# A layernorm's casts moved from GpSimd to ScalarE, and a broadcast copy from ScalarE to VectorE

## The reference

```python
def attn(x):                       # phi(y) = elu(y) + 1, heads of 64
    q = phi(heads(x @ Wq.T + bq)); k = phi(heads(x @ Wk.T + bk))
    v = heads(x @ Wv.T + bv)
    kv = einsum('bhtd,bhtm->bhdm', k, v)
    z = 1.0 / (einsum('bhtd,bhd->bht', q, k.sum(axis=2) + EPS) + EPS)
    out = einsum('bhtd,bhdm,bht->bhtm', q, kv, z)
    return out @ Wo.T + bo
def ffn(x):                        # weights dequantized by 1/127
    return (silu(x @ wg.T) * (x @ wu.T)) @ wd.T
x = layernorm(x + attn(x))         # mean, variance over 1024 features
x = layernorm(x + ffn(x))
```

## Time and profile before

| | |
|---|---|
| median of 2 runs | 5113.15 us (5107.51 to 5118.79) |
| profiled execution, its time | 5102.1 us |
| profiled execution, span of the slowest core (4) | 5100.2 us |
| spans of the 8 cores | 5089.6 to 5100.2 us |
| busy share of the span | PE 72%, DVE 34%, ACT 18%, POOL 11% |
| mean granted clock of PE | 0.83 of 2.4 GHz |

### The profile page before, as it was taken

How to read it: one execution, slowest core, us unless ns; L and a number is a source line. 1 busy time by engine, 2 the same in 40 slices (tenths; PEclk the granted TensorE clock), 3 DMA queues, 4 the chain that set the end, 5 groups by cost and what they waited for, 6 DMA issues and landing times.

```text
span 5100.2 us, 43631 instructions; the slowest of 8 cores (5089.6 to 5100.2 us)
## 1 busy us (share of the span) xinstructions
PE 3689.1 (72%) x15184; PEld 1435.9 (28%) x15184; DVE 1708.7 (34%) x2435; ACT 931.7 (18%) x1659; POOL 554.6 (11%) x668
## 2 busy tenths in 40 slices
PE   1587647677655876799964877699973877699982
PEld 0232212222211322244421322244430322244430
DVE  0124422222232144333333133433333134433333
ACT  2232211011111232111111232111111232211111
POOL 0003210000021013100011012200012012200002
PEclk9787768888877977899976977799985987799995
DMA  4100022222212000010102000010103000001001
GB/s 161 40 0 1 1 74 75 75 75 75 72 49 84 1 1 0 25 50 25 50 33 99 1 1 1 25 50 26 50 10 122 1 1 0 25 26 50 26 25 66
DMA packets 69676, 199.99 MB, mean 39 GB/s; under 512 B 4933, under 2 KB 4934, under 8 KB 60248
## 3 DMA queue, kind: packets, MB, share of 16 engines
q1 hardware_dynamic: 56504, 153.15, 8.5%
q10 hardware_dynamic: 12960, 44.05, 2.5%
HBM read 144.75 MB, written 52.43 MB: 39 GB/s over the span
## 4 chain that ended last, share of the span: by engine, by line
PE 59%; DVE 13%; ACT 8%; DMA 7%; POOL 7%; issue 5%; DVEq 0%; ACTq 0%; SPq 0%; POOLq 0%
PE ps L774 13%; PE ps L753 12%; PE ps L799 12%; PE ps L415 5%; PE ps L620 5%; PE ps L370 4%; DVE x L254 4%; DVE wstage L250 4%; DMA wstage_i<-wu 3%; PE ps L529 3%; POOL arena L189 2%; DMA wstage_i<-wg 2%; POOL arena L187 2%; POOL h_arena L189 1%; DVE h_arena L785 1%
## 5 line engine op out<-in xcount | busy, mean ns | idle before, releaser
L753 PE MATMUL ps<-y_bf,arena 128*128 128x512 bf16 x3072 | 710.3, 388 | 181.9 <-POOL arena L722 74.5
L774 PE MATMUL ps<-y_bf,arena 128*128 128x512 bf16 x3072 | 706.0, 387 | 106.4 <-DVE arena L722 106.4
L799 PE MATMUL ps<-h_arena,arena 128*128 128x512 bf16 x3072 | 694.1, 379 | 35.8 <-DVE h_arena L785 35.8
L785 DVE SCALAR_TENSOR_TENSOR h_arena<-ps,h_arena 128x512 bf16<-128x512 f32 x384 | 265.5, 691 | 1044.9 <-PE ps L774 1041.8
L811 DVE SCALAR_TENSOR_TENSOR x<-ps,x 128x512 f32<-128x512 f32 x768 | 530.2, 691 | 183.6 <-PE ps L799 113.6
L763 ACT ACTIVATE h_arena<-ps 128x512 bf16<-128x512 f32 x384 | 229.1, 597 | 1857.1 <-PE ps L753 1857.1
L415 PE MATMUL ps<-wk_bf,arena 128*128 128x512 bf16 x1024 | 290.4, 433 | 294.2 <-ACT arena L439 177.7
L187 POOL CAST arena<-x 128x512 bf16<-128x512 f32 x160 | 98.2, 614 | 3594.6 <-DVE x L628 1661.6
L753 PEld LDWEIGHTS ps<-y_bf,arena 128*128 128x128 bf16 x3072 | 304.4, 99 | 574.5 <-issue 229.3
L774 PEld LDWEIGHTS ps<-y_bf,arena 128*128 128x128 bf16 x3072 | 303.7, 99 | 493.1 <-issue 144.8
L799 PEld LDWEIGHTS ps<-h_arena,arena 128*128 128x128 bf16 x3072 | 293.7, 98 | 420.6 <-issue 80.4
(11 more groups left out here) (78 smaller groups left out, 2705.8 us busy)
## 6 DMA issues: line engine op xcount, KB each, us to landing
x<-x SPq DMA_DIRECT2D x16, 2048.0 KB, 8.0
out<-x SPq DMA_DIRECT2D x16, 2048.0 KB, 6.9
arena<-stash_wg SPq DMA_DIRECT2D x18, 1024.0 KB, 4.8
arena<-stash_wd SPq DMA_DIRECT2D x18, 1024.0 KB, 6.9
arena<-stash_wu ACTq DMA_DIRECT2D x18, 1024.0 KB, 4.8
wstage_i<-wg SPq DMA_DIRECT2D x48, 256.0 KB, 2.7
wstage_i<-wd ACTq DMA_DIRECT2D x48, 256.0 KB, 2.6
wstage_i<-wu SPq DMA_DIRECT2D x48, 256.0 KB, 2.6
```

What stands on the lines that cost most here:

```text
L753: e.matmul(ps[b_][:, 0:512], slots[sl_][:, 512 * kk + 128 * gg:512 * kk + 128 * (gg + 1)], y_bf[:, T * kk + t_:T * kk + t_ + 512], start=( ...
L774: e.matmul(ps[b_][:, 0:512], slots[sl_][:, 512 * kk + 128 * gg:512 * kk + 128 * (gg + 1)], y_bf[:, T * kk + t_:T * kk + t_ + 512], start=( ...
L785: e.scalar_tensor_tensor(h_arena[:, 512 * gg:512 * (gg + 1)], ps[b_][:, 0:512], S127, h_arena[:, 512 * gg:512 * (gg + 1)], ALU.mult, ALU.m ...
L799: e.matmul(ps[b_][:, 0:512], slots[sl_][:, 1024 * ss + 128 * mm:1024 * ss + 128 * (mm + 1)], h_arena[:, 512 * ss:512 * (ss + 1)], start=(s ...
```

## The change

Three operations move to another engine, and the waits with them.

- The cast of the statistics (one of the two POOL operations for each chunk, in LN1 and LN2) becomes an ACT copy. It has its own waits on DVE and on PE, and PE waits for ACT as well as for POOL.
- The cast to y_bf in LN1 becomes an ACT copy. The wait of PE on POOL ahead of the FFN is taken out; PE waits for ACT there already.
- The copy of the broadcast z from bank 3 to SBUF becomes a DVE copy. PE's next broadcast waits for DVE instead of ACT, and bank 3 is handed to the next tile's Q projection by DVE's count.

```diff
             for m in range(NCH):
                 sa, sb_ = scr[m % npair]
+                p.wait("scalar", dve, src_ready_dve)
+                p.wait("scalar", pe, hist[m % npair])
+                p.op("scalar", lambda e, mm=m, t_=t0, d_=sa: e.copy(
+                    d_[:, :], x32[:, T * mm + t_:T * mm + t_ + 512]), inc=act)
+                cst = act.n
                 p.wait("gpsimd", dve, src_ready_dve)
                 p.wait("gpsimd", pe, hist[m % npair])
-                p.op("gpsimd", lambda e, mm=m, t_=t0, d_=sa: e.tensor_copy(
-                    d_[:, :], x32[:, T * mm + t_:T * mm + t_ + 512]))
                 p.op("gpsimd", lambda e, mm=m, t_=t0, d_=sb_: e.tensor_mul(
...
+                p.wait("tensor", act, cst)
                 p.wait("tensor", pool, sq)
...
                 if want_ybf:
-                    p.wait("gpsimd", dve)
-                    p.op("gpsimd", lambda e, mm=m, t_=t0: e.tensor_copy(
+                    p.wait("scalar", dve)
+                    p.op("scalar", lambda e, mm=m, t_=t0: e.copy(
                         y_bf[:, T * mm + t_:T * mm + t_ + 512],
-                        x32[:, T * mm + t_:T * mm + t_ + 512]), inc=pool)
+                        x32[:, T * mm + t_:T * mm + t_ + 512]), inc=act)
...
                     p.wait("tensor", act, z_ready)
-                    p.wait("tensor", act)
+                    p.wait("tensor", dve, zb_ps3_free)
...
-                    p.wait("scalar", pe, zmm)
-                    p.wait("scalar", dve, zb_free[c % 2])
-                    p.op("scalar", lambda e, cc=c:
-                         e.copy(zb[cc % 2][:, :], ps[3][:, 0:512]), inc=act)
-                    zev = act.n
+                    p.wait("vector", pe, zmm)
+                    p.wait("vector", dve, zb_free[c % 2])
+                    p.op("vector", lambda e, cc=c:
+                         e.tensor_copy(zb[cc % 2][:, :], ps[3][:, 0:512]),
+                         inc=dve)
+                    zev = dve.n
+                    zb_ps3_free = dve.n
...
-                    p.wait("vector", act, zev)
+                    p.wait("vector", dve, zev)
...
-                q_free[3] = act.n
+                q_free_d[3] = zb_ps3_free
...
-            p.wait("tensor", pool)
```

More of the change, by code:

```diff
@@ L500, in build_nc @@
             a_mult = [0] * NCH
+            zb_ps3_free = 0
             stats_free = kv_ready
```

## The result

The changed kernel takes 5028.9 us (median of 11 runs) where the kernel before takes 5183.9 (10 runs). The ratio is 0.979, with a 95% interval from 0.975 to 0.983. That is clearly faster, but the interval holds 0.98, so these runs do not settle whether it is by more than 2%. The spans of single cores are the sharper measure: in the profiled executions core 0 took 5099.0 us before and 4978.7 after, 120 us less, a ratio of 0.976.

A forecast was written before the change was run, and what follows sets the result against it. Serial stretches on other engines while PE stands still were taken as the bound. Terms -72.3 - 62.1 + 12.8 + 21 - 7.1 = -107.7 us take the profiled 5102.1 to 4994, the median 5113 to 5005; 8-in-10 range 4972 to 5042.

The forecast's parts named there:

- The bound: Whole kernel: PE stands still in stretches paced by a serial walk over other engines, such as POOL's layernorm statistics.
- Statistics, LN2: Layernorm behind the FFN, 16 times: casts on ACT shorten the statistics from 13.74 to 9.22 us, saving 72.3 us.
- rival C: Statistics: ACT's cast slows POOL's multiply to 1.93 us, about +110 us in all, 5223; chance 0.05.
- rival D: Statistics gain nothing, chunks staying 1.55 us apart by an unseen limit; +26.7 us, 5140; chance 0.04.
- Statistics, LN1: Layernorm behind the attention, 16 times: statistics take 9.86 us with two scratch pairs, saving 3.88 each, 62.1 in all.
- The ring's arithmetic: LN1's two scratch pairs: multiply m waits until PE has read pair m-2; long matmuls make two chunks take 2.30 us.
- The copy of z: Chunk loop, 128 copies: DVE's copy takes 0.69 us, a step 1.56 instead of 1.46; +12.8 us.
- Rival A: DVE's z copy runs as from SBUF, 0.43 us; sum -140.5, 4972; chance 0.07.
- The hand-over: Apply's start to next tile's denominators: y_bf casts on ACT delay the Q projection, +1.75 us, 12 times, +21.
- Rival B: Next tile's Q projection gets no cover under the apply: +8.6 instead of +1.75, 82 us more, 5087; chance 0.05.
- The FFN's start: Apply's start to FFN's first matmul: 13.5 instead of 15.27 us, saving 1.77, 4 times, 7.1.

The follow-up runs named there:

- denser statistics in the kernel before: Kernel before with one more matmul, result unused, for each chunk of the statistics, POOL still doing both operations; core 0 took 5106.3 us against 5103.
- the pause filled: Changed kernel with 30 more matmuls, results unused, at each of the 12 hand-overs; core 0 took 4956 us, 27 less than the changed kernel.

## Why the prediction was off, and what of it held

**The bound.** Right. The statistics stood on the path in all 32 layernorms, and a cast taken off POOL shortened the path by its whole spacing: a chunk takes 1.00 us instead of 1.55.

**Statistics, LN2.** The spacing of two multiplies was taken as 0.99 and is 0.99 to 1.00; the multiply beside ACT takes 1.039 us, so rival C (ACT and POOL hinder each other) fell, and rival D too. The mis-sized term is the 1.25 us between the last multiply's end and ACT's read. It was read from a tile with long matmuls and kept; it measured 0.83, in all 16 tiles. The spacing, slightly above 0.99, takes some of this back, and 16 times 0.36 us is the 5.8 us that this term missed.

**Statistics, LN1.** This is the step that failed: "I take the first four starts at the short spacing and the rest at the long one". The ring's arithmetic was right (2.30 said, 2.35 measured; the four tiles in which it bound took 10.1 us on the mean), but the length of the matmuls was copied from the kernel before, where they came two to each 1.55 us. With a chunk a microsecond PE has more to do in the same time, and in 12 of 16 tiles the matmuls stayed short to the end. The denser statistics in the kernel before show that more work on PE by itself makes tiles stay or turn short; why it was 12 tiles and not 16 stays open. A saving of 3.88 us a tile was expected, 4.60 measured: 11.5 us in all, the largest miss of the sum.

**The copy of z.** Right in size: 0.69 was taken, 0.691 measured. The step was 1.52 instead of 1.56: the copy starts 0.70 us after its broadcast (median), where 0.73 was taken. Rival A (0.43 us) fell. The page VectorE: DVE Perf Modes of the Trainium skill, section Why PSUM operands drop a tier, gives f32 from PSUM no fast mode, and the 691 ns agree. The cost table of that page of the Trainium skill would have put the copy at 658 ns, an estimate, which is 33 ns short.

**The hand-over.** Right in mechanism: PE restarted 14.65 us after the apply's start (14.67 said), the projection split 32 and 32 with a pause of 6.5 to 7.4 us (near 8 said). The size was +2.37 instead of +1.75, and the term that was too small is what the pause adds to the matmuls behind it: 3.0 or 1.4 us over 6.92 was taken, 2.1 on the mean of the 12, and it measured 2.7 (9.66 us). The prediction paired the longer and the shorter of today's two kinds of restart with the same kind after the change; measured, 11 of the 12 lie from 23.7 to 24.9 and one at 23.0, where before 5 of the 12 were of the longer kind (22.6 to 22.9) and 7 of the shorter (21.1 to 21.6). The bounds given there, +0.5 and +3.2, don't follow from its own terms either: without long matmuls 14.67 + 6.92 = 21.6 is 0.5 less than the mean of 22.1, and with twice as many it is 26.0, 3.9 more. With the pause filled 21.76 was measured. Rival B (no cover at all) fell.

**The FFN's start.** Right: 13.77 for 13.5 said, and the load of the up weights stayed covered: PE waits for no DMA at the up matmuls (line 780).

**The total.** The ratio of 0.979 is what was said (4994 over 5102), but that agreement is partly luck. On core 0 the change gave 120 us and not 107.7, and even this holds two errors that work against each other: 17.3 us too little from the statistics, both times because long matmuls were carried over from the kernel before, and 7.4 us too little for the hand-over.

**Who slows whom.** POOL's multiply is 1039 ns beside ACT's casts, and DVE's line 258 fell back to 692 ns with POOL idle beside it, from 784 before (the mean of LN1 and LN2, line 254 there). With the y_bf cast left on POOL the apply in LN1 stayed at 14.2 us; with that cast alone on ACT it was 12.69. The page SBUF — State Buffer of the Trainium skill, section Who interferes with whom, gives VectorE and GpSimd one shared pair of ports and ScalarE ports of its own; the slowing seen here agrees.

## What to carry to other kernels

When two operations stand one behind the other on one engine, on a path for which everything else waits, and a second engine is idle there, moving the shorter one saves its whole spacing; this was worth 147 us of 5107, and each of the two moves beside it cost 10 to 17. Before a piece of work goes to "an idle engine", ask what stands behind it in that engine's order: each y_bf cast takes ACT 0.62 us, the next tile came 2.4 us later, and with the same casts placed behind the next tile's chunk loop the hand-over was 20.39 us, shorter than the 21.95 of the kernel before. And when matmuls follow one another more closely than before, don't copy their length from the kernel in which they were sparse.

## What the runs showed of the hardware

In the statistics, PE's granted clock went with how closely its matmuls came. With two for each 1.55 us it was 0.50, the lower level of 1.2 GHz, to the end of every tile of LN2, and the matmuls took 0.59 to 0.63 us. With two for each 1.00 us, or three for each 1.55, it went to 1.00, the upper level of 2.4 GHz, within the first six chunks of each, and they took 0.38. The same spacing did not always hold it: in 4 of 16 LN1 tiles of the changed kernel it fell with the multiplies a microsecond apart, and no run shows why in those. Matmuls whose results nobody reads are therefore not always lost: 30 of them in each pause of 6.5 to 7.4 us kept the clock at 1.00, made the next 32 take 7.07 us instead of 9.66 on the mean, and gave 27 us of the whole. But a higher mean clock by itself is no gain: it rose from 0.831 to 0.861 with the denser statistics in the kernel before, and the time stayed.
